# An attention and projection layer on one core: maxima of the first iteration inside the projection's last chunk, earlier weight loads, memory shared between phases

## What is computed

```python
qkv = hidden_states @ Wqkv                     # 32 query heads of 32, one key head, one value head
scores = jnp.where(causal, q.k * scale + slopes * (pos_k - pos_q), NEG_INF)
attn = softmax(scores) @ v
x = _layernorm(x + attn @ Wo)
w = weight + (quantize_dequantize(weight) - weight)   # groups of 128, int4
x = _layernorm(x + einsum('bsd,od->bso', x, w) + bias)
```

## Time and profile before

| | us |
|---|---|
| median of 3 runs | 2347.76 |
| lowest, highest | 2347.06, 2350.14 |
| the profiled execution: its time | 2347.64 |
| its span in the trace | 2345.9 |
| PE busy in the span | 2267.1 (97%) |
| DVE busy | 1606.7 (68%) |
| ScalarE busy | 996.6 (42%) |
| GpSimd busy | 906.3 (39%) |

### The profile page before, as it was taken

One profiled execution on the slowest core, in us unless ns is written; L12 is line 12 of the kernel. 1 busy time (PEld: TensorE's weight loads), 2 busy tenths in 40 slices (PEclk: granted clock), 3 DMA queues, 4 the chain that ended last, 5 costly groups with the idle time before them and its releaser, 6 DMA issues. The chain is left out here.

```text
span 2345.9 us, 37013 instructions
## 1 busy us (share of the span) xinstructions
PE 2267.1 (97%) x12600; PEld 1538.3 (66%) x12600; DVE 1606.7 (68%) x4666; ACT 996.6 (42%) x1944; POOL 906.3 (39%) x559
## 2 busy tenths in 40 slices
PE   7999999869999999999999999997999999999997
PEld 5788888645555555555555555535888888888886
DVE  5777777657777877787878787843655555565564
ACT  3222222137777777777777777771111101011010
POOL 0000000007777777777878787870010101101010
PEclk9999999959999999999999999998999999999999
DMA  6454445474333233323332333237232333323320
GB/s 225 157 175 172 169 174 184 148 160 160 92 88 75 70 92 87 81 64 92 88 85 61 91 87 92 53 118 203 81 107 81 97 94 85 98 83 105 94 67 27
DMA packets 176819, 255.97 MB, mean 109 GB/s; under 512 B 15118, under 2 KB 104846, under 8 KB 176162
## 3 DMA queue, kind: packets, MB, share of 16 engines
q1 hardware_dynamic: 176176, 253.69, 37.3%
q10 hardware_dynamic: 498, 0.49, 0.1%
HBM read 166.04 MB, written 87.03 MB: 108 GB/s over the span
## 5 line engine op out<-in xcount | busy, mean ns | idle before, releaser
L1008 DVE CUSTOM_DVE_ANT_0 unused<-pa,distance 128x512 bf16<-128x512 f32 (+3 forms) x1536 | 772.5, 554 | 238.1 <-PE pa L845 212.8
L986 ACT ACTIVATE probs<-pa,slope 128x512 f32<-128x512 f32 (+3 forms) x1536 | 765.6, 592 | 259.9 <-PE pa L868 119.8
L823 POOL TENSOR_TENSOR probs<-probs 128x1024 f32<-128x1024 f32 x252 | 673.5, 2673 | 86.3 <-ACT probs L986 63.4
L845 PE MATMUL pa<-k,ff_hi 96*128 96x512 f32 (+1 forms) x1008 | 319.4, 374 | 23.6 <-DMA ff_hi<-q_lo_d 20.2
L1237 POOL TENSOR_TENSOR yb<-y,bias 128x1024 f32<-128x1024 f32 x32 | 76.6, 2394 | 655.4 <-DVE z L1260 631.0
L882 PE MATMUL pa<-probs,v 128*32 128x512 f32 (+3 forms) x3072 | 300.7, 494 | 1.2 <-issue 0.8
L868 PE MATMUL pa<-ff_hi,k 116*128 116x512 f32 (+1 forms) x798 | 300.0, 415 | 0.1
L845 PEld LDWEIGHTS pa<-k,ff_hi 96*128 96x128 f32 x1008 | 185.8, 193 | 142.5 <-DVE mx L1008 86.6
L809 POOL TENSOR_SCALAR_AFFINE_SELECT probs<-probs 128x512 f32<-128x512 f32 x256 | 158.7, 637 | 192.9 <-ACT probs L986 192.9
L1201 ACT ACTIVATE ln<-ln 128x1 f32<-128x1 f32 x64 | 13.0, 203 | 498.2 <-DVE ln L1280 498.2
L302 PE MATMUL ps<-xt_hi,wq_hi 128*128 128x512 f32 (+1 forms) x552 | 220.7, 400 | 2.8 <-DVE k_lo L511 2.8
(11 more groups left out here) (120 smaller groups left out, 3018.2 us busy)
## 6 DMA issues: line engine op xcount, KB each, us to landing
ff_hi<-q_hi_d SPq DMA_DIRECT2D x84, 256.0 KB, 5.6
x_in<-in_L_attn_hidden_states SPq DMA_DIRECT2D x8, 2048.0 KB, 9.1
q_hi_d<-q_hi SPq DMA_DIRECT2D x64, 256.0 KB, 2.0
q_lo_d<-q_lo SPq DMA_DIRECT2D x64, 256.0 KB, 2.4
att_d<-att SPq DMA_DIRECT2D x64, 256.0 KB
x_in<-in_L_attn_hidden_states SPq DMA_DIRECT2D x32, 512.0 KB, 3.8
out<-z SPq DMA_DIRECT2D x32, 512.0 KB, 2.6
k<-k_d SPq DMA_DIRECT2D x32, 384.0 KB, 7.9
```

Source lines behind the costliest of these rows:

```text
L823: nc.gpsimd.tensor_tensor(o, o, probs[:, source % PR, h0:h1, 0:N], ALU.add).then_inc(add_done, 1)
L845: nc.tensor.matmul(bank[:, 0:keys], q3[u][0:3 * D, qb // BPH, h, qb % BPH * P:(qb % BPH + 1) * P], k3[u][0:3 * D, k0:k0 + keys], start=Tru ...
L986: nc.scalar.activation(probs[:, n % PR, h, 0:N], sc_ps[sc_ring.bank[use]][:, at:at + N], ACT.Exp, scale=slope[:, bass.ds(g * HPG + h, 1)]) ...
L1008: nc.vector.tensor_tensor_reduce(out=unused[:, use % MXB, 0:keys], in0=bank[:, 0:keys], in1=distance[:, d0:d0 + keys], scale=1.0, scalar=- ...
```

## The change

- The maxima of iteration 0 (48 pieces and two turns) are made by PE and DVE within the projection's last chunk: between the weight tiles of products 4 to 8, one or two pieces behind every third matmul, in two PSUM banks. Their queries and keys are loaded at the start of that chunk (`load_first`), and half of iteration 1's later in it (`load_second`).
- The product of keys and values takes the high and low halves of its weights side by side as one weight of 128 columns (`wkv`), against the high and low half of x: 16 matmuls in place of 24. ScalarE copies one half of the result, DVE adds the two halves for k (`kv`) and for v (`vt`); vt was a ScalarE copy before.
- `group_scales` of the next chunk moves from product 0 of that chunk to product 8 of the chunk before; the Wf block's load moves forward to after product 6 (7 in chunk 0). In chunk 0 Wo's split moves behind product 2 and the turn of the quantized block behind product 8. In the last chunk the quantization is pressed into products 0 to 3 and the turn goes behind product 6.
- x and its halves, distance, maxima, the first queries and keys, and later memory of the finish share one place (`Shared`).
- The constant rows of queries and keys are rounded once by ScalarE at the kernel's start, written to DRAM (`rows_d`) and loaded from there. Before, ScalarE copied them into all three slots at the start of attend.
- The projection's loops are written out.

The core of the diff (moved helper functions that keep their work are left out):

```diff
+FIRST = [("piece", n) for n in range(20)] + [("turn", 0)] + [("piece", n) for n in range(20, len(PIECES))] + [("turn", 1)]
...
+        FIRST_FROM = MM - 5
+
+        def first_uses(c, k):
+
+            begin, end = (min(12 * (c - FIRST_FROM) + 3 * n // 2, len(FIRST) - 1) for n in (k, k + 1))
+            return range(len(FIRST) - 1, len(FIRST)) if (c, k) == (MM - 1, 3) else range(begin, end)
...
+            def load_first():
+                sp.wait_ge(tr_done, tr_uses(NCH - 2, TR_X + KT - 1))
+                sp.wait_ge(mm_done, (NCH - 1) * MM)
...
+                sp.dma_start(raw(sh.k3[0][0:3 * D, :]), k_d[:, 0:S]).then_inc(sh.loaded[0], 16)
+                load_queries(sp, first_q, q_hi_d, q_lo_d, 0, sh.loaded[0])
+                sp.dma_start(sh.distance, distance_h).then_inc(sh.distance_in, 16)
...
+                    if c == (6 if first else 5) and not last:
+
+                        sp.wait_ge(quant_steps, t * QSTEPS + QSTEPS)
+                        sp.dma_start(stage[:, W_STAGE:W_STAGE + 1, 0:H], w_blk[:, bass.ds(t + 1, 1), :]).then_inc(w_loaded, 16)
...
+                    if last and c == 1:
+                        load_second()
+                    if last and c == QC - 2:
+                        store_wf(t)
+                        for half in range(HALF):
+                            put_max(sp, sh, first_q, 0, half, FIRST.index(("turn", half)) + 1)
...
+                with_maxima = t == NCH - 1 and c >= FIRST_FROM
+                if with_maxima and c == FIRST_FROM:
+                    pe.wait_ge(sh.loaded[0], LOADS - 16)
                 for k in range(KT):
+                    last = weight_tile(u, c, k)
+                    if with_maxima and k < KT - 1:
+                        for use in first_uses(c, k):
+                            first_maximum(use)
...
+            def first_maximum(use):
+
+                if use >= 2:
+                    pe.wait_ge(sh.mx_free, use - 1)
...
+                terms = ((wq_hi, xt_hi), (wq_hi, xt_lo), (wq_lo, xt_hi)) if c else ((wkv, xt_hi), (wkv, xt_lo))
...
-                    if c == 7:
+                    if c == (8 if first else 6 if last else 7):
                         pe.wait_ge(quant_steps, t * QSTEPS + QSTEPS)
...
+                    if last and c >= FIRST_FROM:
+                        dve.wait_ge(sh.distance_in, 16)
+                        for use in (use for k in range(KT) for use in first_uses(c, k)):
+                            take_maximum(nc, dve, sh, 0, FIRST[use], first_ps[use % 2], use, sh.unused[:, use % 2, :])
                     if c == 0:
+                        dve.wait_ge(kv_part, t + 1)
                         dve.wait_ge(kv_stored, t * 64 + CREDIT)
-                        nc.vector.tensor_tensor(k_lo[:, :], bank[0:D, :], raw(k_hi[:, :]), ALU.subtract).then_inc(mm_free, 1)
+                        nc.vector.tensor_tensor(kv[0:D, :], bank[0:D, :], kv[0:D, :], ALU.add).then_inc(k_sum, 1)
+                        nc.vector.tensor_tensor(vt[:, :], bank[D:2 * D, :], kv[D:2 * D, :], ALU.add).then_inc(vt_ready, 1)
+                        dve.wait_ge(mm_hi, t * MM + c + 1)
+                        nc.vector.tensor_tensor(k_lo[:, :], kv[0:D, :], raw(k_hi[:, :]), ALU.subtract).then_inc(mm_free, 1)
...
+                    if c == MM - 1 and not last:
+                        group_scales(t + 1)
+                    if last:
+                        if c == 0:
+                            quotients(t, 0, True)
+                        elif c == 1:
+                            quotients(t, 0, False)
+                            quotients(t, 1, True)
+                        elif c == 2:
+                            quotients(t, 1, False)
+                        elif c == 3:
+                            fake_quantized(t)
```

More of the change, by code:

```diff
@@ new lines, in put_max, with make_maximum @@
+def put_max(sp, sh, q, t, c, turned):
+    sp.wait_ge(sh.mx_free, turned)
+    if t < SLOTS:
+        sp.wait_ge(sh.rows_in[t], 16 * (HALF + 1))
+    for row, half in ((3 * D + 2, sh.mxt_hi), (3 * D + 3, sh.mxt_lo)):
+        sp.dma_start(raw(q[c][row:row + 1, :, :]).rearrange("r h q -> r (h q)"), raw(half[:, c, :])).then_inc(sh.neg_max[t % SLOTS][c], 16)
+def make_maximum(nc, pe, sh, w, item, bank, q, k, ready):
+    kind, m = item
+    if kind == "piece":
+        _, h, qb, k0, keys = PIECES[m]
+        nc.tensor.matmul(bank[:, 0:keys], q[qb // BPH][0:3 * D, h, qb % BPH * P:(qb % BPH + 1) * P], k[0:3 * D, k0:k0 + keys],
+                         start=True, stop=True).then_inc(sh.mx_done, 1)
+        return
+    if m == 0:
+        pe.wait_ge(sh.mx_free, ready)
+        src = sh.mx[:, 0:BPH * HPG]
+    else:
+        pe.wait_ge(sh.mx1_done, w + 1)
+        src = sh.mx1[:, :]
+    nc.tensor.transpose(bank[0:BPH * HPG, 0:P], src, sh.ident[:, :]).then_inc(sh.mx_done, 1)
@@ L255, in body @@
                     sp.dma_start(k_d[row:row + D, tok], raw(half[:, :])).then_inc(kv_stored, 16)
[L256 to L260, removed]
+                if not first:
+                    store_wo(t)
                 for c in range(QC):
@@ L312, in first_products @@
                             pe.wait_ge(mm_free, mm_ring.free(0, c))
-                        cols = slice(NH * D, QKV) if c == 0 else slice((c - 1) * P, c * P)
-                        o = mm_ps[mm_ring.bank[c]][0:cols.stop - cols.start, :]
-                        for n, (w, xt) in enumerate(((wq_hi, xt_hi), (wq_hi, xt_lo), (wq_lo, xt_hi))):
-                            last = nc.tensor.matmul(o, w[:, k, cols], xt[:, 0, k, :], start=(k == 0 and n == 0),
-                                                    stop=(k == KT - 1 and n == 2))
+                        last = weight_tile(0, c, k)
                         if k == KT - 1:
@@ L336, in body @@
             def body(t, u, i):
[L337 removed]
+                first, last = t == 0, t == NCH - 1
                 pe.wait_ge(tr_free, t * TR + (KT + TR_X + KT))
@@ L382, in body @@
                 nc.scalar.copy(wo_hi[:, :], stage[:, WO_STAGE, 0:H]).then_inc(wo_hi_done, 1)
+            def body(t, u, i):
+                first, last = t == 0, t == NCH - 1
+                if not first:
+                    split_wo(t)
                 for c in range(MM):
@@ L595, in attend @@
     plan = [step.split() for step in plan]
-    assert sum(step.count("M") for step in plan) == len(pieces)
+    assert sum(step.count("M") for step in plan) == len(PIECES)
     pool_order = [
```

441 lines of the change are left out of this document (233 added, 208 removed).

## The result

The changed kernel takes **2337.74 us** (median of six runs, 2334.94 to 2340.19) against 2347.41 for the kernel before (2345.94 to 2350.14): ratio 0.9956, 95% interval 0.9944 to 0.9968. It is faster by 0.44%, 9.7 us. The forecast was 2313.4, with a range from 2300 to 2324: the sign is right, the size is not. The profiled run took 2334.94 (span 2333.2), 12.7 us less than the profiled run before; the working forecast 34.2. So **21.5 us are missing**, and most of this document is about where they went.

The account below looks back on a forecast made before the run. PE was taken as the bound, so shortening its stream or idle stretches counts. Up to the last chunk 15.0 us and in the last chunk with its seam 19.2 sum to 34.2; 2347.64 becomes 2313.4, range 2300 to 2324.

Parts of the forecast that it names:

- Matmuls taken out: Projection's key and value product: 16 matmuls instead of 24, 1.81 us less in each of 8 chunks.
- rival (d): Projection: wider weight loads are not hidden, so 14.5 us come back, 2327.9; chance 0.02.
- Start and chunk 0: Kernel start to chunk 0's end: earlier first products, shorter waits; chunk 1 starts at 75.5 against 85.11, -9.6 us.
- Chunk 1: After product 1, PE stalls 3.9 us for vt (bounds 0 and 7), Wf landing taken as 3.6; net +3.7 us.
- Chunks 2 to 6: Projection: five chunks each 1.81 us shorter, -9.1 us; wait for v zero, bounds 0 to 0.5 a chunk.
- rival (c): Chunks 2 to 7: v's turn waits for DVE behind late scales; 2360 with an 18 us landing; chance 0.02.
- Last chunk: PE waits about 13 us in product 4 for DVE's quantization; scores at +81.4 against +100.6, -19.2 us.
- (a): Last chunk: the cover holds, DVE is not in PE's way; 2298.6; chance 0.08.
- (b): Last chunk: clock stays at half after the stall and into iteration 0; +25 us, 2338; chance 0.05.
- Iteration 0: First attention iteration: left at its 36.2 us at a clock of 0.81, since the idle seam drops the clock as before.
- (e): Both stalls as forecast, but iteration 0 starts at full clock; -3 us, 2310; no separate chance given.
- The finish: End of the kernel: it keeps its chain, so its change was put at zero.

Follow-up runs that it names:

- experiment 4: Changed kernel, maxima from product 5 of the last chunk instead of 4: 2334.11 us; separately, without quantizing the last 128 rows of Wf (output differs): 2328.97 us.
- experiment 2: Changed kernel, Wo's 8 MB loaded in slices in iterations 2 to 17: 2328.08 us; instead kept in iteration 0 behind the first half's maxima rows: 2342.43 us.
- the profile with 64 bytes: Changed kernel with 64 unused bytes in each partition between the shared buffers and everything allocated after them: 2336.64 us.
- The 128 bytes: Changed kernel with 128 unused bytes in each partition between the shared buffers and everything allocated after them: 2330.25 us, ratio 0.9923 to the kernel before.

## Why the prediction was wrong, point by point

- **Matmuls taken out: right.** 1.81 us a chunk were forecast. With all tiles at the same phase, chunks come 52.28 apart against 54.1 to 54.7 before, 1.9 under the lowest. Wide weight loads are not in the open, and rival (d) is out. The rule of the Trainium skill, page "TensorE: Matmul & The Clock Gate", section "LDWEIGHTS (loading the stationary operand)", by which a load's time goes by its columns (P/1.2 ns), is borne out here in the difference: the traces record 134 ns for a load of 64 columns and 188 for one of 128, 54 apart where the rule gives 53, but not half and double. The spacing shows that such loads cost nothing here behind matmuls of 512 columns.
- **Start and chunk 0: right.** The first products end at 35.46 (forecast 34.8), k_lo wait 1.50 (1.4), wait for the quantized block 0.55 (under 1), the chunk's end 0.6 us late. The clock loss of 1.6 us behind the k_lo wait did not come (full clock from 23.44 to 88.30); VectorE's block came later than PE anyway.
- **Chunk 1: mechanism right, the landing mis-sized.** "With no stores beside it I take 3.6": it was 6.4, within the bound of 6.8 that I had beside it, and there were stores beside it: four of q, 256 KB each, issued from 75.95 to 78.44. The row of the page said 6.8; I argued myself away from it. Putting the scales back gives 8.4 us.
- **Chunks 2 to 6: order right, pitch wrong.** No wait for vt came back, so rival (c) is out. But each chunk of the xq and xk halves is longer, by 208 matmuls of 4.7 ns, 1.0 us (0.8 of it in one spacing of the rows above, the rest in its neighbour), which I had not looked for: I took the pitch of 0.227 from a kernel whose buffers all lay alike and did not ask what the new memory plan does.
- **Last chunk: the stall right, the total partly by luck.** Pieces start at +34.8 as forecast (435.79, just ahead of the matmul at 436.14), a wait of 12.74 (13), clock back at 439.87, bank waits 0.9 (4 were forecast), scores at +81.9 (+81.4), seam 4.94 (5.0). From the end of the wait to the last matmul's end it is 41.6 us (41.2). Less 0.9 of waits and an estimated 1.9 of clock (3.73 us at half), PE's own work took 38.8 where I had 35.5: 3.3 us too little there and 3.1 too much for the banks nearly cancel. Rivals (a) and (b) are out. The sign "clock 5 tenths in a slice near 430" was badly chosen: half clock lasted 13.65 us (426.22 to 439.87), and a slice of 58 us shows 8. What was missed is the second bound under the first (experiment 4).
- **Iteration 0: this step failed.** "I leave iteration 0 at its 36.2 us" looked at its clock only. The change moves the loads of v, of half of the second iteration's queries and of the row constants to its start, ahead of Wo's 8 MB on the sync engine's queue. Every moved transfer had to be counted on that queue, and the cover there (PE waited 0.81 before, so it had none) had to be named. It cost 7.7 us in iteration 0 and, by the half clock behind the wait, 0.8 in iteration 1 (33.9 instead of the forecast 33.1); experiment 2 gives 9.7 back. The clock did start at half, as before (0.56 up to 500), so (e) did not come here. In the profile with 64 bytes it nearly did (full clock after 3.6 us) and gave nothing, for the rows ended the iteration.
- **The finish: this step failed too.** "The finish keeps its chain; I put it at zero." Its chain is the same, its operands' addresses are not: 6.2 us more. The 128 bytes give 6.6 back, and the 1536 products with Wf at 4.0 ns more each make 6.1.
- **The wait ahead of the finish** grew from 12.0 to 13.5. It is 12.4 to 14.2 in the variants of the changed kernel; I have no cause for these 1.5 us.

Together the two failed steps and the pitch of the chunks make 7.7 + 6.2 + 2.2 = 16.1 of the 21.5 us, the landing in chunk 1 another 2.3. The range of 2300 to 2324 had no term that made iteration 0 or the finish longer: what was put at zero had no bounds on that side.

## What to carry to other kernels

When loads are moved ahead of time, list what stands behind them on their new place of the queue and when each of those is needed; a small transfer that has just been on time is the first to be late. A large load of no urgency is better sent in slices, in iterations with room for them, than at once. When a change shares or moves buffers, treat the memory plan as part of the change: compare the start-to-start time of the same matmuls by operand before anything else is blamed.

## What the runs showed of the hardware

- Behind a matmul of 128 x 512 whose loaded and streamed tiles begin at different bytes modulo 256 in the partition (0 and 128), the next one starts 4 to 5 ns later than with equal phases: 232 against 227 ns in the projection, 231.9 against 227.9 in the finish. It holds whichever tile is at 0 (pad in front), vanishes with 128 bytes between and not with 256, and appears in the kernel before when 128 bytes are put in. A difference of 64 showed as 0.2 us between two chunk spacings of the projection instead of 0.8, and cost the full amount in the finish; that asymmetry is not explained.
- On the sync engine's queue a transfer was late by what stood ahead of it: a store of 256 KB took 10.5 us behind 2.4 MB of loads and 1.2 MB of stores (2.4 at the median), and two rows of maxima took 10.9 us behind 8 MB issued 23 us ahead of them (513.96 to 524.89), 2.4 without the 8 MB. The second 4 MB landed after 32.6 us when 1.6 MB more stood before them, 27.4 without.
- The same instructions at the start of iteration 0, behind an idle stretch of PE of 5 to 6 us, ran at half clock for 15.0 us in the changed kernel and for 3.6 in the one with 64 bytes.
- A load of 512 KB that the change left without cover took 6.4 us from issue (76.79) to the first instruction that reads it (83.18), with 1 MB of stores issued around it.
